# Final stage of an audio tower: where the low parts of its weights are made, and when GpSimd's bias additions begin

## The reference, cut to what matters

```python
h = h + _L1_ffn_ref(_layernorm(h, axis=-1), W, b, Wq, Wk, A, Bm)

def _L1_ffn_ref(x, W, b, Wq, Wk, A, Bm):      # E, DK, R = 8, 32, 16
    result = jnp.einsum('bsi,oi->bso', x, W) + b
    q = jnp.einsum('bsi,ni->bsn', x, Wq).reshape(Bt, S, E, DK)
    k = jnp.einsum('bsi,ni->bsn', x, Wk).reshape(Bt, S, E, DK)
    w = jax.nn.softmax(jnp.einsum('bsed,bsed->bse', q, k) / math.sqrt(DK), axis=-1)
    h = jnp.einsum('bsi,eri->bser', x, A)
    return result + jnp.einsum('bse,bser,eor->bso', w, h, Bm)
```

## Time and profile before

| | us |
|---|---|
| median of 3 runs (lowest to highest) | 3009.76 (3008.11 to 3013.42) |
| the profiled execution, its own time | 3008.69 |
| its span in the trace | 3007.0 |
| TensorE busy in the span | 2797.8 |
| VectorE, ScalarE, GpSimd busy | 1781.2, 985.2, 129.9 |

### The profile page before, as it was taken

How to read it: one execution, slowest core, us unless ns; L and a number is a source line. 1 busy time by engine, 2 the same in 40 slices (tenths; PEclk the granted TensorE clock), 3 DMA queues, 4 the chain that set the end, 5 groups by cost and what they waited for, 6 DMA issues and landing times. The chain is left out here.

```text
span 3007.0 us, 37373 instructions
## 1 busy us (share of the span) xinstructions
PE 2797.8 (93%) x13193; PEld 2280.7 (76%) x13193; DVE 1781.2 (59%) x3197; ACT 985.2 (33%) x2026; POOL 129.9 (4%) x76
## 2 busy tenths in 40 slices
PE   7994899999899999989999998999999888749999
PEld 6772688888788888877888887888888766548888
DVE  4887565566665555667665566766556556563322
ACT  3453333333333323333333234333323324431110
POOL 2110000000000000000000000000000000241100
PEclk9996899999999999999999999999999998979999
DMA  5320322223222222312222221222222111010000
GB/s 111 77 57 0 113 75 78 76 73 98 63 92 77 77 77 77 98 61 81 91 77 77 77 83 57 96 94 77 77 77 77 56 57 42 1 71 22 29 28 29
DMA packets 55468, 207.19 MB, mean 69 GB/s; under 512 B 6784, under 2 KB 7168, under 8 KB 53312
## 3 DMA queue, kind: packets, MB, share of 16 engines
q1 hardware_dynamic: 55360, 205.79, 21.5%
HBM read 197.37 MB, written 8.39 MB: 68 GB/s over the span
## 5 line engine op out<-in xcount | busy, mean ns | idle before, releaser
L987 PE MATMUL at_proj<-qr_xhi,at_whi 128*128 128x512 f32 x1536 | 628.5, 409 | 13.2 <-DVE at_wlo L869 8.8
L989 PE MATMUL at_proj<-qr_xhi,at_wlo 128*128 128x512 f32 x1536 | 602.5, 392 | 0.0
L988 PE MATMUL at_proj<-qr_xlo,at_whi 128*128 128x512 f32 x1536 | 601.1, 391 | 0.0
L987 PEld LDWEIGHTS at_proj<-qr_xhi,at_whi 128*128 128x128 f32 x1536 | 290.2, 189 | 77.0 <-DVE at_wlo L869 9.4
L988 PEld LDWEIGHTS at_proj<-qr_xlo,at_whi 128*128 128x128 f32 x1536 | 290.5, 189 | 63.5 <-issue 7.5
L989 PEld LDWEIGHTS at_proj<-qr_xhi,at_wlo 128*128 128x128 f32 x1536 | 289.5, 188 | 63.7
L1032 PE MATMUL at_out<-at_wohi,at_ohi 128*128 128x512 f32 x1008 | 312.2, 391 | 6.2 <-DVE at_wolo L874 4.2
L1032 PE MATMUL at_out<-at_wohi,at_olo 128*128 128x512 f32 x1008 | 311.3, 390 | 0.0
L1032 PE MATMUL at_out<-at_wolo,at_ohi 128*128 128x512 f32 x1008 | 311.2, 390 | 0.0
L744 ACT COPY at_pT<-at_tp 128x512 f32<-128x512 f32 x128 | 75.2, 588 | 598.5 <-PE at_tp L1008 598.5
L865 DVE TENSOR_TENSOR at_olo<-at_ov,at_ohi 128x512 fp32r<-128x512 f32 x128 | 88.5, 692 | 307.0 <-ACT at_ohi L749 307.0
(11 more groups left out here) (238 smaller groups left out, 4215.9 us busy)
## 6 DMA issues: line engine op xcount, KB each, us to landing
at_wstage<-in_w_qkv_dram SPq DMA_DIRECT2D x192, 512.0 KB, 3.6
at_ostage<-in_w_o_dram SPq DMA_DIRECT2D x128, 512.0 KB, 4.5
cv_x<-in_x_dram SPq DMA_DIRECT2D x32, 512.0 KB, 6.7
out_dram<-h SPq DMA_DIRECT2D x16, 512.0 KB, 2.6
fn_w_lo_raw<-in_w_t_dram SPq DMA_DIRECT2D x8, 512.0 KB, 7.1
fn_qka_lo_raw<-in_qka_t_dram SPq DMA_DIRECT2D x5, 512.0 KB, 5.8
sc_fhi_raw<-in_dft_fwd_dram SPq DMA_DIRECT2D x4, 512.0 KB, 7.8
sc_chi_raw<-in_lag_cos_dram SPq DMA_DIRECT2D x2, 512.0 KB, 9.9
```

The source lines that it names most:

```text
L987: pe.matmul(proj[:, j % 2, :], hi[:, w], x_hi[:, k, :], start=(k == 0), stop=False)
L988: pe.matmul(proj[:, j % 2, :], hi[:, w], x_lo[:, k, :], start=False, stop=False)
L989: last = pe.matmul(proj[:, j % 2, :], lo[:, w], x_hi[:, k, :], start=False, stop=(k == KT - 1))
```

## The change

GpSimd no longer makes any low part. VectorE makes all fourteen, in the order in which TensorE asks for them: those of `qka` behind the first group's statistics, then `x_lo` of tile 0, all eight of `w`, and that of `bm`. GpSimd begins its bias additions when the low part of `bm`, the last of the fourteen, is there.

```diff
             @block.gpsimd
             def _(pool):
-                qka.low(pool)
-                w.low(pool, range(KT // 2))
 
                 pool.wait_ge(bias_in, 16)
+                bm.ready(pool)
                 with pool.Fori(0, NB) as t:
                     after(pool, rows.normed, t + 1)
                     pool.tensor_tensor(row(h, t), row(h, t), bias_row[:, :], ALU.add).then_inc(biased, 1)
...
             def _(dve):
                 def before():
                     rows.stats(dve, 0, range(GROUP))
+                    qka.low(dve)
                     rows.low(dve, 0, 0)
-                    w.low(dve, range(KT // 2, KT))
+                    w.low(dve)
                     bm.low(dve)
```

## The result

| | before | after |
|---|---|---|
| median of the runs (lowest to highest), us | 3010.97 (3008.11 to 3013.42), 4 runs | 2990.68 (2987.51 to 2994.36), 4 runs |
| profiled execution, its own time and span, us | 3008.69, 3007.0 | 2994.36, 2992.6 |

The ratio is 0.9933, with a 95% interval of 0.9916 to 0.9951: 0.67% faster. The forecast was 2992.7 us, in a range of 2990.0 to 2997.5. The medians lie 20.29 us apart; the interval of the ratio stands for some 15 to 25 us.

A forecast was written before the change was run, and what follows sets the result against it. TensorE, busy 2797.8 of 3007.0 us, bounds the kernel, so only its preamble waits and low clock can be won. 15.03 + 1.99 = 17.02 us off 3008.69 gives 2991.67, plus 1.07 to the median: 2992.7 us, range 2990.0 to 2997.5.

The forecast's parts named there:

- the statistics chain freed: Final stage, first group: with GpSimd idle, VectorE's chain takes 3.28 us instead of 9.83, so 6.55 us go.
- five subtractions of `qka`: VectorE makes the five low parts behind the statistics at 1.13 us each, 5.65 us in all.
- queries of tile 0 start: TensorE starts them at 2658.21, right behind x_lo, 5.37 us earlier; 15.08 us into the final stage.
- the low part of `bm` ends: VectorE's last subtraction, behind the eight of w, ends at 2668.33, 25.20 us into the final stage.
- output of tile 0 starts: TensorE starts it at 2668.48 instead of 2683.51, 15.03 us earlier; 25.35 us into the final stage.
- output of tile 0 takes: TensorE's output part takes 12.52 us instead of 14.5, 1.99 less, without the long idleness ahead of it.
- the stretch: From VectorE's first statistics instruction of the final stage to TensorE's first matmul of tile 1's queries: 17.02 us less.
- What the two engines share: VectorE and GpSimd take turns on something shared, so VectorE's 3.36 us subtractions of w would take 1.22 us alone.
- the third rival: w's transfers, not GpSimd, slow the first group's statistics: only 10.5 us won, 2999.3 us; chance 0.05.
- Slow of themselves: Rival: subtractions cost VectorE 3.3 us even without GpSimd; tile 0's output starts 15.3 us later, 3025 us; chance 0.03.
- The bias additions in the gate: GpSimd's additions overlap VectorE's gate of tile 0 at no cost; rival: TensorE loses 2.3 us, 2995.0 us, chance 0.13.
- The clock: TensorE's clock: 1.99 us won in tile 0's output, no change in its queries; rival: not won, 2994.7 us, chance 0.07.

The follow-up runs named there:

- the second execution: The changed kernel, unaltered, measured once more on another chip: ratio to the kernel before 0.9933, median 2988.14 us.
- the run with both: Changed kernel plus chunk 0 of qka on GpSimd, waits for w by chunk, 48 and 20 extra identity transposes: ratio to before 0.9932, median 2989.64 us.

## Why the prediction was right

Its terms, with positions from the start of the stage:

| step | predicted | measured |
|---|---|---|
| the statistics chain freed | 6.55 us | 6.56 (shift ready at 8.15 instead of 14.71) |
| five subtractions of `qka` | 5.65 | 5.69 start to start |
| queries of tile 0 start | 15.08 | 15.15 |
| the low part of `bm` ends | 25.20 | 25.31 |
| output of tile 0 starts | 25.35 | 25.55 |
| output of tile 0 takes | 1.99 less | 2.00 less |
| the stretch | 17.02 less | 16.83 less |

**What the two engines share** was the step on which everything rested, and it was read from ends that coincide. Five runs bear it out: the chain is slow again when only `qka` goes back, the subtractions are at 3.0 us again when only `w` does, two bias additions beside them cost them 3.90 us, and GpSimd's copies, which read SBUF, slow them where its fills do not. What the runs show less of is which instructions of VectorE are concerned. The subtractions read two tensors in SBUF, but the slow instructions of the statistics (128 x 4) and of the gate (128 x 8) are TENSOR_SCALARs that read one, and they waited; the eight statistics instructions read one too and did not. No run here tests what sets these apart.

**The transfers** as the cause of the slow statistics, the third rival, fell with the changed kernel itself. Over the chain w's transfers keep the DMA engines as busy as before (the last two columns are their mean busy share and GB/s), and it takes 3.3 us. Before, for the first 3.3 us of it, and after:

```profile
2648.00:2651.30 3.30, 0.00 (x0) 0.00 (x0) 3.18 (x8) 0.00 (x0) 3.30 (x3) 0.50 1.01 398
2650.50:2653.80 3.30, 0.00 (x0) 0.00 (x0) 2.79 (x20) 0.00 (x0) 0.00 (x0) 0.50 1.03 418
```

**Slow of themselves**, the rival on the other side, fell with 1.22 us a subtraction.

**The bias additions in the gate.** I had put both narrow instructions behind an addition each and found the result just in time. One waits: the 1-wide instruction at 2671.96 takes 0.15 us with an addition under way, only the 8-wide one waits. The result is ready 28.52 us into the stage and asked for at 31.10, so the cover is 2.6 us and not 0.1. The gate's price of nothing was right, for a better reason than mine.

**The clock.** The 2.00 us of the output came, as the rows before had them. The term I set at nothing, the queries, was mis-sized: 5.28 us instead of 4.60, since the clock stayed at its lower level to their end. TensorE's transposes of tile 1 thus ended at 25.79 instead of 24.89, and the output, which starts 0.24 us ahead of that end, at 25.55. So TensorE, not VectorE, set the start of the output. It cost 0.1 us of 17 (38.06 against 37.96 in the second execution), because the two engines were nearly balanced.

**The total.** The forecast of 2992.7 is 2.0 us above the median, which is less than the stages ahead move a single execution by. That it came so close is in part luck: the medians fell by 20.29 us, 3.5 more than the stretch. The stretch, 17.02 forecast and 16.83 measured, is the better test. The comparison of the profiled executions, 14.33 us, is less than the 16.83 of the stretch by just such a difference, 2645.63 - 2643.13 = 2.50 us.

## What to carry to other kernels

Before splitting elementwise work between VectorE and GpSimd, look at what each reads: here two engines that each subtracted from SBUF to SBUF took 3.3 us a round, in which VectorE alone would have done nearly three, and GpSimd's long instructions held a serial chain of tiny ones as well. GpSimd's share was free beside the eight statistics instructions, and its fills, which read nothing, were free beside the subtractions; but one tensor in SBUF is no safe sign, since the TENSOR_SCALARs of the chain read one and waited. A wait that keeps GpSimd out of the way was worth 6.6 us here.

When an instruction is far over its usual time, compare its end with the ends on the other engine: a coincidence within 0.1 us, as here, gives a suspect before any run, and taking the other engine away tests it.

Where the stages ahead scatter by more than the gain in question, measure the stretch that the change can touch.

## What the runs showed that I had not expected

TensorE's granted clock does not follow from the length of the pause alone. It was at half for the first 5.9 us of the output behind a pause of 4.67 us (window from 2672.60 to 2678.50) and stayed full behind one of 2.94 us; but in the runs with extra transposes it stayed full behind one of 1.78 us and fell about 1 us after one of 2.28 us (the run with both), in the midst of a row of transposes with no pause between them. And one program, with the same pause of 3.69 us ahead of its queries, had them at 0.50 once and at a mean of 0.66 another time. What decides it these runs don't settle.

The start of the final stage moves by 8.3 us (2638.99 to 2647.32) between executions with the same code ahead of it. I did not look for the cause.
